# Turning the selected z by 32x32 blocks on VectorE, in a routed feed-forward kernel with split-precision products

## The chip, the cores and the metric

The kernel runs on one core of one Trainium2 chip. The metric is the device time of one execution in microseconds (us). The kernel before takes 426.58 us, the median of three runs (425.37 to 426.68).

## The reference, cut to what matters

```
W = weights[condition]                          # 64 matrices of 64 x 64, picked by index
y = einsum('bct,bcd->bdt', x, W)                # x: (64, 64, 1024), fp32
logits = y @ gate_w.T + expert_bias             # 4 experts
one_hot = one_hot(argmax(logits), 4)
z = einsum('nh,erh->ner', y, lora_A)            # 4 experts x rank 8 = 32 values for each row
delta = one_hot-selected (z @ lora_B[e].T)      # rank 8, the chosen expert alone
out = x + y @ W_up.T + delta
```

There are 4096 rows of 1024 values. For each row the kernel keeps of its 32 values of z the 8 of the best expert and sets the others to zero. The product with the four experts' `lora_B`, laid side by side as 32 rows, is then the delta.

## The kernel before, in words

**Tiling.** A tile is 128 rows, two batches of 64. A block q is two tiles, t = 0 and 1, and there are 16 blocks. Each block is a 2 x 2 x 2 product of halves (two tiles by two halves of the hidden size), done with seven products in place of eight, named after their stationary operand: a11, a12, a22, s2, s1, s3, s4. Each product is made with both operands split into a rounded high part and a low part, and three of the four part products are summed in PSUM, so a product has 12 matmuls of 512 columns or 24 of half as many. In the odd blocks the product a22 is itself split into seven quarter products, which take a22 of the even block before with them (`q1` to `q4`, and `q_of_sum` for 5, 6 and 7).

**Who does what.** TensorE makes y of the next block (`make_y`, L785) and the products (L869, L1071). ScalarE moves y out of PSUM (L524) and rounds the high parts (L533). GpSimd forms sums of operands (L304 to L317). VectorE forms the low parts (L289, and L1427 for quarter products), adds the products to x (L1264, L1268, L1458), and routes. SyncE loads and stores.

**Routing.** The gate's 4 columns and `lora_A`'s 32 are carried as extra columns in four products. When the tile's 36 columns are there, VectorE runs `route(q, t)`: `find_best` (L1221), `rank_best` (L1225), `find_first` (L1230), `select_z` (L1234, which writes `z_sel`, 128 rows x 32). `high_z` (L1247) writes the rounded z to parts 0 and 2 of `z_parts`, and `low_z` (L1251) z less its high part to parts 1 and 3. Each step waits for the one before on the semaphore `route_step`. TensorE turns `z_parts` (128 x 128) into a PSUM bank in `turn_z` (L884), and ScalarE copies it to `z_t[t]` (`move_z` L611, in block 0 also `move_first_z` L601). `z_t[t]` is the stationary operand of the low-rank matmuls (L875): `delta11_of` and `delta12_of` for t = 0, `second_delta` for t = 1. This happens 32 times, once for each tile.

**What sets the order.** The order of each engine's instructions is written out by hand, and semaphores join the engines. Every engine runs its own list in order. The lists are `one` for block 1, `even` for blocks 2, 4, ..., 14, `odd` for blocks 3, 5, ..., 13 and `odd` with `closing` for block 15 (on TensorE `close`). Block 0 is written out by itself, since it is mixed with the preparation of the weights.

On TensorE an even block runs a11, a12, s2, y, the turn of t = 0, s1, delta11, y, s3, y, s4, delta12, the turn of t = 1, y, second_delta. An odd block runs a11, q2, a12, q1, q5, s2, q6, q3, y, s1, the turn of t = 0, q7, delta11, y, s3, q4, y, s4, delta12, the turn of t = 1, y, second_delta. The closing block runs the turn of t = 0 and `last_columns(0)` (L1147, with s4's first columns) after q3; then delta11, s3, q7, s1, the turn of t = 1, q4, second_delta, `last_columns(1)`.

On VectorE, in an odd block, these stand around `route(q, 0)`:

```
drain(3, g, bank_b, 1, 1, 6)
route(q, 0)
after_p6(q, 1)
low_quarter(7, g)
low_operand(dve, "s4", a12, q)
```

and in the closing block `route(q, 0)` is followed by `low_operand(dve, "s4", a12, q)`, and `route(q, 1)` by `drain(7, g, bank_c, 3, 1, 5)`. TensorE's q7 waits for `low_quarter(7)`, `last_columns(0)` for the low part of s4, and q4 for `drain(7)`.

In block 0 VectorE runs after `route(0, 0)` the low parts `low_sum(1, 3)`, a11, `low_sum(4, 3)` and `low_sum(1, 1)`, and TensorE's product s1 waits for both of the `low_sum(1, ...)`. GpSimd has then its own two low sums to finish and goes on to `add_s1` and `add_s2` of block 1, for which it waits on ScalarE's last copies of y, and one of these stands behind `move_first_z` in ScalarE's list.

Of the kernel before, what the change touches and what calls it, by code (L numbers as in the profile page):

```python
# [5 lines left out]
def adaln_ffn_kernel(  # L6
# [39 lines left out]
    P = 128  # L46
# [10 lines left out]
    WARM_UP = 62  # L57
    ROUTE_STEPS = 7
    assert C == D and 2 * D == P and HALF == BANK and O == T and BLOCKS % 2 == 0
# [9 lines left out]
    with ctx:  # L69
# [117 lines left out]
        route_step = sem("route_step")  # L187
        z_turned = sem("z_turned")
        z_ready = sem("z_ready")
        delta11 = sem("delta11")  # L190
# [318 lines left out]
        def _(act):  # L509
# [88 lines left out]

            def move_first_z(src):
                act.wait_ge(z_turned, 1)  # L600
                act.activation(z_t[0][:, :], src, ACT.Copy).then_inc(z_ready, 1)  # L601
# [5 lines left out]
            def move_z(q, par, t, bank):  # L607
                act.wait_ge(z_turned, 2 * q + t + 1)
                if not (isinstance(q, int) and q == 0):
                    act.wait_ge(delta22 if t else delta12, q)  # L610
                act.activation(z_t[t][:, :], bank[:, 0:P], ACT.Copy).then_inc(z_ready, 1)  # L611

# [65 lines left out]
            move_first_y(3, 1, a22)  # L678
            move_first_z(y_ps[:, 1, 0:P])
            act.wait_ge(low["s4"], 1)  # L680
            move_first_y(2, 1, a12)
            move_z(0, 0, 1, chains[1][:, 1, :])
            act.wait_ge(y_summed, Y_AT[2, 1])
# [24 lines left out]
            def one(q):  # L708
                load_x(q + 1, 0, 0)
                round_s1(q, True)  # L710
                round_s2(q, True)
                load_x(q + 1, 0, 1)
                round_s4(q, True)
                round_s3(q, True)
                move_z(q, 1, 0, bank_c[:, 0, :])
# [6 lines left out]
                move_z(q, 1, 1, chains[0][:, 1, :])  # L722
                round_fine(5)
                round_fine(7)
                round_fine(6)
                act.wait_ge(product_done["a22"], 2)
                act.wait_ge(rebuilt, 4)
                round_fine(4)
                move_y(q + 1, 1, 1, a22_even)

            def even(q, g):
                load_x(q + 1, 1, 0)
                round_s1(q, True)
                round_s2(q, True)
# [4 lines left out]
                move_z(q, 0, 0, bank_c[:, 0, :])  # L739
# [6 lines left out]
                move_z(q, 0, 1, chains[1][:, 1, :])  # L746
                move_y(q + 1, 1, 1, a22)

            def odd(q, g, closing):
# [14 lines left out]
                move_z(q, 1, 0, y_ps[:, 1, :])  # L764
                if not closing:
# [3 lines left out]
                    move_y(q + 1, 1, 0, a21)  # L769
                move_z(q, 1, 1, chains[0][:, 1, :])  # L770
                if not closing:
# [6 lines left out]
        def _(pe):  # L778
# [128 lines left out]
            def first_delta21():  # L907
                add_delta_pair(1, bank_x).then_inc(delta21, 1)

            def turn_second_z(q, pair):  # L910
                pe.wait_ge(c11_out, q + 1)
                turn_z(pair[:, 1, 0:P], q, 1)

# [78 lines left out]
            multiply_half("s3", 1, bank_x, False)  # L992
            wait_piece_read("b21", 2)
            turn_z(y_ps[:, 1, 0:P], 0, 0)
            wait_y_moved(3, 1)
# [8 lines left out]
            multiply("s1", 0, bank_b, True)  # L1004
            turn_second_z(0, bank_y)
            wait_sums(4, 0)
            wait_sums(4, 1)
            last_product(0, bank_x)
            pe.wait_ge(z_ready, 2)
            first_delta22()  # L1010
            pe.wait_ge(z_ready, 2)
            first_delta21()


            def one(q):
# [9 lines left out]
                make_y(q + 1, 0, 0, 0)  # L1025
                pe.wait_ge(p4_out, q)
                turn_z(bank_c[:, 0, 0:P], q, 0)
                pe.wait_ge(c22_out, q)
# [4 lines left out]
                multiply("s3", q, chain, False)  # L1033
                make_y(q + 1, 0, 1, 0)
                multiply("s4", q, bank_c, True)
                delta12_of(q)
                turn_second_z(q, pair)
                make_y(q + 1, 0, 1, 1)
# [3 lines left out]
            def even(q, g):  # L1042
# [7 lines left out]
                make_y(q + 1, 1, 0, 0)  # L1050
                pe.wait_ge(c12_out, q)
                turn_z(bank_c[:, 0, 0:P], q, 0)
                pe.wait_ge(c22_out, q)
# [4 lines left out]
                multiply("s3", q, chain, False)  # L1058
                make_y(q + 1, 1, 1, 0)
                multiply("s4", q, bank_c, True)  # L1060
                delta12_of(q)
                turn_second_z(q, pair)
                make_y(q + 1, 1, 1, 1)
# [51 lines left out]
            def odd(q, g, closing):  # L1115
# [7 lines left out]
                multiply("s1", q, bank_b, True)  # L1123
                pe.wait_ge(y_summed, 4 * q + 4)
                turn_z(y_ps[:, 1, 0:P], q, 0)
                pe.wait_ge(quarter_out, quarters(g, 6))
# [10 lines left out]
                delta12_of(q)  # L1137
                turn_second_z(q, pair)
                make_y(q + 1, 0, 1, 1)
# [3 lines left out]
            def last_columns(n):  # L1143
                dst, cols = y_ps[:, n, 0:QUARTER], slice(n * QUARTER, (n + 1) * QUARTER)
                for k in range(KH):
                    for a, b in ((0, 0), (0, 1), (1, 0)):
                        mm = pe.matmul(dst, hl["s4"][:, a, k, :], w_of["s4"][:, b, k, cols],  # L1147
                                       start=(k == 0 and a + b == 0), stop=False, skip_group_check=True)
                pe.wait_ge(z_ready, 2 * LAST + 1)
                add_delta(0, dst, lora_b_hl[:, BANK + n * QUARTER:BANK + (n + 1) * QUARTER]).then_inc(delta12, 1)  # L1150

            def close(q, g, chain, pair):
                pe.wait_ge(y_summed, 4 * q + 4)
                turn_z(y_ps[:, 1, 0:P], q, 0)
                pe.wait_ge(low["s4"], q + 1)
# [7 lines left out]
                multiply("s1", q, bank_b, True)  # L1163
                turn_second_z(q, pair)
                pe.wait_ge(quarter_out, quarters(g, 7))
# [9 lines left out]
        def _(dve):  # L1175
# [63 lines left out]

            def twice(z):  # L1240
                return z[:, :].unsqueeze(1).to_broadcast([P, 2, ER])
# [12 lines left out]
            def route(q, t, used=True):  # L1254
# [5 lines left out]
                high_z(n, used or t)  # L1260
                low_z(n)

# [16 lines left out]

            def after_p2(q, par, used=True):  # L1280
                score_p2(q, par)
                route(q, 0, used)

# [79 lines left out]
            score_p2(0, 0)  # L1363
            route(0, 0, False)
            low_sum(dve, 1, 3)
# [184 lines left out]
```

## Time and profile before

| | before |
|---|---|
| median of three runs | 426.58 us |
| lowest and highest | 425.37, 426.68 us |
| span of the profiled execution, first to last instruction | 423.9 us |
| whole time of the profiled execution | not reported apart; the median lies 2.7 us above the span |
| TensorE busy | 414.2 us, 3003 matmuls |
| VectorE busy | 280.3 us, 605 instructions |
| ScalarE busy | 146.0 us, 282 instructions |
| GpSimd busy | 137.3 us, 123 instructions |
| mean granted TensorE clock | 0.996 |

Busy time is the time in which the profile has at least one instruction of an engine at work. The times of instructions overlap: a matmul's record holds its whole way through the array, so the next one starts before it ends. The cost of a matmul in a stream is therefore the distance between two starts, not its duration.

### The profile page before, as it was taken

The page shows a single profiled execution, that of the slowest core. Times are in us where ns is not written, and L with a number is a line of the kernel's source. Part 1 is how long each engine was busy: PE and PEld are TensorE (multiplying, and loading weights), DVE is VectorE, ACT ScalarE, POOL GpSimd, SP SyncE. Part 2 cuts the span into 40 slices and gives each one's busy share as a digit, 9 for nine tenths or more (in the row PEclk, how much of TensorE's full clock was granted, in tenths as well). Part 3 has the DMA queues.
Part 4 walks back from the last instruction along what each step waited for, and adds up shares of the span by engine and source line. Part 5 has one row for each costly group of instructions (what it writes and reads, how often), then busy time and mean ns, then how long its engine had stood idle before and what let it go on. Part 6 is the DMA issues. An engine that isn't in the chain of part 4 may idle for free.

```text
span 423.9 us, 8776 instructions
## 1 busy us (share of the span) xinstructions
PE 414.2 (98%) x3003; PEld 393.6 (93%) x3003; DVE 280.3 (66%) x605; ACT 146.0 (34%) x282; POOL 137.3 (32%) x123
## 2 busy tenths in 40 slices
PE   7998999999999999999999999999999999999997
PEld 6897998999999999999999999999999999999996
DVE  4699668586756576474675656575764756856684
ACT  5795222433223242232333233232332323323320
POOL 1488215506204080312605053050802216050430
PEclk9899999999999999999999999999999999999999
DMA  8820230503114032321125021150322212240102
GB/s 269 302 65 2 89 117 26 178 27 106 67 57 159 26 107 100 105 76 74 56 99 176 28 102 38 65 179 25 105 97 82 99 55 75 99 177 29 49 26 100
DMA packets 20991, 39.36 MB, mean 93 GB/s; under 512 B 7494, under 2 KB 7750, under 8 KB 20970
## 3 DMA queue, kind: packets, MB, share of 16 engines
q1 hardware_dynamic: 17600, 27.40, 18.3%
q10 hardware_dynamic: 3370, 11.69, 8.1%
q8 instruction: 12, 0.20, 0.2%
q14 instruction: 9, 0.07, 0.1%
HBM read 22.30 MB, written 16.78 MB: 92 GB/s over the span
## 4 chain that ended last, share of the span: by engine, by line
PE 92%; DVE 3%; DMA 1%; ACT 1%; SPq 1%; issue 1%; POOL 1%; ACTq 0%; POOLq 0%
PE bank_y L869 21%; PE bank_x L869 21%; PE y_ps L785 11%; PE bank_b L869 10%; PE bank_c L869 10%; PE bank_c L1071 5%; PE bank_b L1071 4%; DMA x_sb<-in_x_dram 1%; PE bank_x L849 1%; PE y_ps L794 1%; PE bank_x L875 1%; PE bank_b L875 1%; PE bank_y L875 1%; PE bank_c L875 1%; PE y_ps L1147 1%
## 5 line engine op out<-in xcount | busy, mean ns | idle before, releaser
L524 ACT ACTIVATE a<-y_ps 128x512 f32<-128x512 f32 x49 | 29.3, 598 | 93.4 <-PE y_ps L785 93.4
L785 PE MATMUL y_ps<-cond_pair,x_sb 128*128 128x128 f32 x448 | 59.0, 274 | 0.0
L785 PEld LDWEIGHTS y_ps<-cond_pair,x_sb 128*128 128x128 f32 x448 | 54.7, 191 | 1.2
L869 PE MATMUL bank_y<-w_s,hl_s 128*128 128x292 f32 (+1 forms) x384 | 51.4, 289 | 0.0
L869 PE MATMUL bank_x<-w_a,hl_a 128*128 128x256 f32 (+1 forms) x384 | 50.9, 288 | 0.0
L869 PEld LDWEIGHTS bank_x<-w_a,hl_a 128*128 128x128 f32 x384 | 49.5, 188 | 0.3
L304 POOL TENSOR_TENSOR s_sum<-a 128x512 f32<-128x512 f32 x9 | 11.6, 1291 | 117.3 <-ACT a L524 115.1
L869 PEld LDWEIGHTS bank_y<-w_s,hl_s 128*128 128x128 f32 x384 | 49.2, 188 | 0.1
L869 PE MATMUL bank_b<-w_s,hl_s 128*128 128x512 f32 x192 | 47.9, 398 | 0.0
L869 PE MATMUL bank_y<-w_a,hl_a 128*128 128x292 f32 x360 | 47.7, 288 | 0.0
L869 PEld LDWEIGHTS bank_y<-w_a,hl_a 128*128 128x128 f32 x360 | 46.6, 188 | 0.3
L869 PE MATMUL bank_x<-w_s,hl_s 128*128 128x292 f32 x336 | 45.2, 290 | 0.4 <-DVE hl_s L289 0.4
L304 POOL TENSOR_TENSOR s_sum<-a,a_even 128x512 f32<-128x512 f32 x7 | 9.0, 1291 | 112.4 <-ACT a_even L524 112.4
L869 PE MATMUL bank_c<-w_s,hl_s 128*128 128x512 f32 x180 | 45.0, 398 | 0.0
L869 PEld LDWEIGHTS bank_x<-w_s,hl_s 128*128 128x128 f32 x336 | 43.0, 188 | 0.6 <-issue 0.6
L869 PEld LDWEIGHTS bank_b<-w_s,hl_s 128*128 128x128 f32 x192 | 35.0, 188 | 6.9
L869 PEld LDWEIGHTS bank_c<-w_s,hl_s 128*128 128x128 f32 x180 | 32.7, 188 | 6.6 <-issue 0.2
L289 DVE TENSOR_TENSOR hl_s<-s_sum,hl_s 128x512 fp32r<-128x512 f32 x30 | 36.3, 1246 | 1.2 <-ACT hl_s L533 1.2
L289 DVE TENSOR_TENSOR hl_a<-a,hl_a 128x512 fp32r<-128x512 f32 x31 | 21.3, 689 | 18.9 <-ACT hl_a L533 18.9
L533 ACT ACTIVATE hl_s<-s_sum 128x512 fp32r<-128x512 f32 x32 | 20.2, 634 | 34.1 <-POOL s_sum L304 24.7
L1264 DVE TENSOR_TENSOR x_sb<-bank_y,x_sb 128x512 f32<-128x512 f32 x40 | 27.3, 682 | 6.0 <-PE bank_y L875 4.8
L533 ACT ACTIVATE hl_s<-a 128x512 fp32r<-128x512 f32 x32 | 19.3, 628 | 33.4 <-POOL a L312 22.5
(187 smaller groups left out, 648.3 us busy)
## 6 DMA issues: line engine op xcount, KB each, us to landing
out_dram<-x_sb SPq DMA_DIRECT2D x63, 256.0 KB, 2.0
x_sb<-in_x_dram ACTq DMA_DIRECT2D x22, 512.0 KB, 3.5
x_sb<-in_x_dram SPq DMA_DIRECT2D x10, 512.0 KB, 3.4
w_raw<-in_L_ffn_W_up_dram SPq DMA_DIRECT2D x8, 512.0 KB, 6.3
cond_pair<-in_L_cond_weights_dram SPq DMA_DIRECT2D x64, 16.0 KB, 2.2
out_dram<-x_sb SPq DMA_DIRECT2D x2, 128.0 KB, 2.0
router_sb<-in_L_ffn_lora_A_dram ACTq DMA_DIRECT2D x1, 128.0 KB
lora_b_sb<-in_L_ffn_lora_B_dram SPq DMA_DIRECT2D x1, 128.0 KB, 4.9
```

The lines of the kernel that those rows point to most:

```text
L289: eng.tensor_tensor(hl[op][:, 1, :, :], by_k(src[:, :]), hl[op][:, 0, :, :].bitcast(fp32), ALU.subtract)\
L304: eng.tensor_tensor(s1_sum[:, :], a21[:, :], second[:, :], ALU.add).then_inc(s1_added, 1)
L524: act.activation(to[:, :], y_ps[:, h, :], ACT.Copy).then_inc(y_summed, 1)
L533: act.activation(hl[op][:, 0, :, :], src[:, :].rearrange("q (k n) -> q k n", n=P), ACT.Copy)\
L785: mm = pe.matmul(y_ps[:, h, k * P:(k + 1) * P], x_sb[:, 2 * par + t, (h * KH + k) * P:(h * KH + k + 1) * P], cond_pair[:, 2 * par + t, :], ...
L794: mm = pe.matmul(first_y_bank(t, h)[:, k * P:(k + 1) * P], x_sb[:, t, (h * KH + k) * P:(h * KH + k + 1) * P], cond_pair[:, t, :], start=Tr ...
L849: mm = pe.matmul(dst, hl[op][:, a, k, :], w_of[op][:, b, k, cols], start=(fresh and k == 0 and a + b == 0), stop=(k == KH - 1 and a == 1), ...
L869: mm = pe.matmul(dst, hl[op][:, a, k, :], w[:, b, k, cols], start=(fresh and k == 0 and a + b == 0), stop=(k == KH - 1 and a == 1), skip_g ...
L875: return pe.matmul(dst, z_t[t][:, :], src, start=False, stop=True, skip_group_check=True)
L1071: mm = pe.matmul(bank[:, 0, 0:QUARTER], left[:, a, k, :], right[:, b, k, :], start=(fresh and k == 0 and a + b == 0), stop=(k == 1 and a = ...
L1147: mm = pe.matmul(dst, hl["s4"][:, a, k, :], w_of["s4"][:, b, k, cols], start=(k == 0 and a + b == 0), stop=False, skip_group_check=True)
L1264: return dve.tensor_tensor(wide(x_part(par, t, half)), bank[:, :, 0:QUARTER], wide(x_part(par, t, half)), ALU.add)
```

## The change

The block `z_rows` (32 x 128) takes the place of `z_parts` (128 x 4 x 32). VectorE turns the four 32 x 32 blocks of `z_sel` into `z_rows`, one instruction each. It then copies `z_rows` to partitions 0 to 31 and 64 to 95 of `z_t[t]` and writes the difference to partitions 32 to 63 and 96 to 127. TensorE's transposes of z, ScalarE's copies and their two semaphores are gone. TensorE waits for `route_step` right before the low-rank matmuls. Two waits on a free bank that stood before a turn (`p4_out`, `c12_out`) stand now before the product s4, which writes the same bank.

```
-    ROUTE_STEPS = 7
+    ROUTE_STEPS = 8
...
-        z_parts = sb("z_parts", [P, 4, ER], fp32)
+        z_rows = sb("z_rows", [ER, P], fp32)
...
-            def turn_z(dst, q, t):
+            def wait_z(q, t):
                 pe.wait_ge(route_step, ROUTE_STEPS * (2 * q + t + 1))
-                pe.transpose(dst, z_parts[:, :, :].rearrange("p n q -> p (n q)"), ident[:, :]).then_inc(z_turned, 1)

             def delta11_of(q, pair):
-                pe.wait_ge(z_ready, 2 * q + 1)
+                wait_z(q, 0)
                 add_delta_pair(0, pair).then_inc(delta11, 1)
...
             def second_delta(q, chain):
-                pe.wait_ge(z_ready, 2 * q + 2)
+                wait_z(q, 1)
...
-            def high_z(n, used):
-                dve.wait_ge(route_step, ROUTE_STEPS * n + 5)
-                if used:
-                    dve.wait_ge(z_turned, n)
-                dve.tensor_copy(z_parts[:, 0:4:2, :].bitcast(fp32r), twice(z_sel)).then_inc(route_step, 1)
-
-            def low_z(n):
+            def z_part(t, n):
+                return z_t[t][n * ER:(n + 1) * ER, :]
+
+            def turn_z(n):
+                dve.wait_ge(route_step, ROUTE_STEPS * n + 5)
+                for i in range(P // ER):
+                    turned = dve.transpose(z_rows[:, i * ER:(i + 1) * ER], z_sel[i * ER:(i + 1) * ER, :])
+                turned.then_inc(route_step, 1)
+
+            def high_z(q, t, n):
                 dve.wait_ge(route_step, ROUTE_STEPS * n + 6)
-                dve.tensor_tensor(z_parts[:, 1:4:2, :], twice(z_sel), z_parts[:, 0:4:2, :], ALU.subtract)\
+                if not (isinstance(q, int) and q == 0):
+                    dve.wait_ge(delta22 if t else delta12, q)
+                dve.tensor_copy(z_part(t, 0), z_rows[:, :])
+                dve.tensor_copy(z_part(t, 2), z_rows[:, :]).then_inc(route_step, 1)
+
+            def low_z(t, n):
+                dve.wait_ge(route_step, ROUTE_STEPS * n + 7)
+                dve.tensor_tensor(z_part(t, 1), z_rows[:, :], z_part(t, 0).bitcast(fp32), ALU.subtract)
+                dve.tensor_tensor(z_part(t, 3), z_rows[:, :], z_part(t, 0).bitcast(fp32), ALU.subtract)\
                    .then_inc(route_step, 1)
```

The calls of `turn_z` on TensorE and of `move_z` and `move_first_z` on ScalarE are taken out, and `route` calls the new `turn_z` on VectorE between `select_z` and `high_z`.

## Rows read from the trace of the kernel before

**Rows 1.** The page: span, then busy time, share and instructions of each engine.

```profile
span 423.9 us, 8776 instructions
...
PE 414.2 (98%) x3003; PEld 393.6 (93%) x3003; DVE 280.3 (66%) x605; ACT 146.0 (34%) x282; POOL 137.3 (32%) x123
```

**Rows 2.** TensorE's waits: releaser, us in total, times, longest.

```profile
PE bank_x L884 <- DVE z_parts L1251: 1.1, 1, 1.1
...
PE bank_x L869 <- DVE hl_s L289: 0.4, 1, 0.4
```

**Rows 3.** Timeline, block 4 (even), TensorE: start, duration, engine, line, work.

```profile
135.39 1.05 PE L785 MATMUL y_ps<-cond_pair,x_sb 128*128 128x128 f32 x8
...
136.28 0.27 PE L884 MATMUL bank_c<-ident,z_parts 128*128 128x128 f32 x1
136.31 3.01 PE L869 MATMUL bank_b<-w_s,hl_s 128*128 128x512 f32 x12
```

**Rows 4.** Timeline, block 5 (odd), from y to q7 on both engines.

```profile
161.29 1.05 PE L785 MATMUL y_ps<-cond_pair,x_sb 128*128 128x128 f32 x8
...
162.10 3.01 PE L869 MATMUL bank_b<-w_s,hl_s 128*128 128x512 f32 x12
...
162.46 0.25 DVE L1234 SCALAR_TENSOR_TENSOR z_sel<-ranks,first,scores 128x32 f32<-128x32 f32 x1
162.75 0.20 DVE L1247 CAST z_parts<-z_sel 128x64 fp32r<-128x64 f32 x1
162.98 0.22 DVE L1251 TENSOR_TENSOR z_parts<-z_sel,z_parts 128x64 f32<-128x64 f32 x1
...
163.12 0.68 DVE L1264 TENSOR_TENSOR x_sb<-bank_y,x_sb 128x512 f32<-128x512 f32 x1
163.72 0.41 DVE L1427 TENSOR_TENSOR hl_q<-a_even,hl_q 128x256 fp32r<-128x256 f32 x1
...
164.98 0.96 PE L1071 MATMUL bank_c<-w_q,hl_q 128*128 128x256 f32 x6
```

**Rows 5.** Timeline, block 4 (even), the end of its second route.

```profile
145.36 0.22 DVE L1251 TENSOR_TENSOR z_parts<-z_sel,z_parts 128x64 f32<-128x64 f32 x1
...
147.37 0.69 DVE L1268 TENSOR_TENSOR x_sb<-bank_c,x_sb 128x512 f32<-128x512 f32 x1 [1.79 <-PE bank_c L875]
...
148.09 0.48 PE L875 MATMUL bank_x<-lora_b_hl,z_t 128*128 128x256 f32 x2
```

**Rows 6.** Timeline, block 0, from the first route to the product s1.

```profile
38.19 1.20 DVE L1247 CAST z_parts<-z_sel 128x64 fp32r<-128x64 f32 x1
...
40.14 3.00 PE L869 MATMUL bank_c<-w_s,hl_s 128*128 128x512 f32 x12
...
41.04 1.29 POOL L304 TENSOR_TENSOR s_sum<-a 128x512 f32<-128x512 f32 x1 [1.71 <-ACT a L528]
41.37 1.51 DVE L268 TENSOR_TENSOR w_s<-t_sb,w_s 128x512 fp32r<-128x512 f32 x1
...
43.44 2.91 PE L869 MATMUL bank_b<-w_s,hl_s 128*128 128x512 f32 x12
```

**Rows 7.** Timeline, block 1, the second route under GpSimd's sums.

```profile
73.22 1.17 DVE L1251 TENSOR_TENSOR z_parts<-z_sel,z_parts 128x64 f32<-128x64 f32 x1
...
74.54 0.30 PE L884 MATMUL bank_x<-ident,z_parts 128*128 128x128 f32 x1 [1.15 <-DVE z_parts L1251]
...
75.49 0.48 PE L875 MATMUL bank_y<-lora_b_hl,z_t 128*128 128x256 f32 x2
```

**Rows 8.** Timeline, block 15 (closing), the two places behind a route.

```profile
408.17 0.69 DVE L289 TENSOR_TENSOR hl_s<-a,hl_s 128x512 fp32r<-128x512 f32 x1
...
409.63 1.67 PE L1147 MATMUL y_ps<-w_s,hl_s 128*128 128x256 f32 x12
...
416.73 0.42 DVE L1458 TENSOR_TENSOR x_sb<-bank_c,x_sb 128x256 f32<-128x256 f32 x1
...
418.01 0.96 PE L1071 MATMUL bank_c<-w_a,hl_a 128*128 128x256 f32 x6
```

More of the change, by code:

```diff
@@ L187, in adaln_ffn_kernel @@
         route_step = sem("route_step")
-        z_turned = sem("z_turned")
-        z_ready = sem("z_ready")
         delta11 = sem("delta11")
@@ L605, in wait_all_turned @@
                 act.wait_ge(piece_stage[b][c], TURNED)
[L607 to L611, printed above, removed]
             act.wait_ge(ident_done, 1)
@@ L678, in _ @@
             move_first_y(3, 1, a22)
-            move_first_z(y_ps[:, 1, 0:P])
             act.wait_ge(low["s4"], 1)
             move_first_y(2, 1, a12)
-            move_z(0, 0, 1, chains[1][:, 1, :])
             act.wait_ge(y_summed, Y_AT[2, 1])
@@ L714, in one @@
                 round_s3(q, True)
-                move_z(q, 1, 0, bank_c[:, 0, :])
                 move_y(q + 1, 0, 0, a11)
@@ L721, in one @@
                 move_y(q + 1, 1, 0, a21)
-                move_z(q, 1, 1, chains[0][:, 1, :])
                 round_fine(5)
@@ L738, in even @@
                 round_even_a22(q, g)
-                move_z(q, 0, 0, bank_c[:, 0, :])
                 move_y(q + 1, 0, 0, a11)
@@ L745, in even @@
                 move_y(q + 1, 1, 0, a21)
-                move_z(q, 0, 1, chains[1][:, 1, :])
                 move_y(q + 1, 1, 1, a22)
@@ L763, in odd @@
                     round_a11(q + 1, True)
-                move_z(q, 1, 0, y_ps[:, 1, :])
                 if not closing:
@@ L769, in odd @@
                     move_y(q + 1, 1, 0, a21)
-                move_z(q, 1, 1, chains[0][:, 1, :])
                 if not closing:
@@ L908, in first_delta21 @@
                 add_delta_pair(1, bank_x).then_inc(delta21, 1)
-            def turn_second_z(q, pair):
-                pe.wait_ge(c11_out, q + 1)
-                turn_z(pair[:, 1, 0:P], q, 1)
             def warm_up(n, bank):
@@ L992, in _ @@
             multiply_half("s3", 1, bank_x, False)
-            wait_piece_read("b21", 2)
-            turn_z(y_ps[:, 1, 0:P], 0, 0)
             wait_y_moved(3, 1)
@@ L1004, in _ @@
             multiply("s1", 0, bank_b, True)
-            turn_second_z(0, bank_y)
             wait_sums(4, 0)
@@ L1008, in _ @@
             last_product(0, bank_x)
-            pe.wait_ge(z_ready, 2)
+            wait_z(0, 1)
             first_delta22()
-            pe.wait_ge(z_ready, 2)
             first_delta21()
@@ L1025, in one @@
                 make_y(q + 1, 0, 0, 0)
-                pe.wait_ge(p4_out, q)
-                turn_z(bank_c[:, 0, 0:P], q, 0)
                 pe.wait_ge(c22_out, q)
@@ L1034, in one @@
                 make_y(q + 1, 0, 1, 0)
+                pe.wait_ge(p4_out, q)
                 multiply("s4", q, bank_c, True)
                 delta12_of(q)
-                turn_second_z(q, pair)
                 make_y(q + 1, 0, 1, 1)
@@ L1050, in even @@
                 make_y(q + 1, 1, 0, 0)
-                pe.wait_ge(c12_out, q)
-                turn_z(bank_c[:, 0, 0:P], q, 0)
                 pe.wait_ge(c22_out, q)
@@ L1059, in even @@
                 make_y(q + 1, 1, 1, 0)
+                pe.wait_ge(c12_out, q)
                 multiply("s4", q, bank_c, True)
                 delta12_of(q)
-                turn_second_z(q, pair)
                 make_y(q + 1, 1, 1, 1)
@@ L1123, in odd @@
                 multiply("s1", q, bank_b, True)
-                pe.wait_ge(y_summed, 4 * q + 4)
-                turn_z(y_ps[:, 1, 0:P], q, 0)
                 pe.wait_ge(quarter_out, quarters(g, 6))
@@ L1137, in odd @@
                 delta12_of(q)
-                turn_second_z(q, pair)
                 make_y(q + 1, 0, 1, 1)
@@ L1148, in last_columns @@
                                        start=(k == 0 and a + b == 0), stop=False, skip_group_check=True)
-                pe.wait_ge(z_ready, 2 * LAST + 1)
+                wait_z(LAST, 0)
                 add_delta(0, dst, lora_b_hl[:, BANK + n * QUARTER:BANK + (n + 1) * QUARTER]).then_inc(delta12, 1)
@@ L1153, in close @@
                 pe.wait_ge(y_summed, 4 * q + 4)
-                turn_z(y_ps[:, 1, 0:P], q, 0)
                 pe.wait_ge(low["s4"], q + 1)
@@ L1163, in close @@
                 multiply("s1", q, bank_b, True)
-                turn_second_z(q, pair)
                 pe.wait_ge(quarter_out, quarters(g, 7))
@@ L1238, in select_z, with route @@
                     op0=ALU.is_equal, op1=ALU.mult).then_inc(route_step, 1)
-            def twice(z):
-                return z[:, :].unsqueeze(1).to_broadcast([P, 2, ER])
-            def high_z(n, used):
+            def z_part(t, n):
+                return z_t[t][n * ER:(n + 1) * ER, :]
+            def turn_z(n):
                 dve.wait_ge(route_step, ROUTE_STEPS * n + 5)
-                if used:
-                    dve.wait_ge(z_turned, n)
-                dve.tensor_copy(z_parts[:, 0:4:2, :].bitcast(fp32r), twice(z_sel)).then_inc(route_step, 1)
-            def low_z(n):
+                for i in range(P // ER):
+                    turned = dve.transpose(z_rows[:, i * ER:(i + 1) * ER], z_sel[i * ER:(i + 1) * ER, :])
+                turned.then_inc(route_step, 1)
+            def high_z(q, t, n):
                 dve.wait_ge(route_step, ROUTE_STEPS * n + 6)
-                dve.tensor_tensor(z_parts[:, 1:4:2, :], twice(z_sel), z_parts[:, 0:4:2, :], ALU.subtract)\
+                if not (isinstance(q, int) and q == 0):
[6 more added lines that the diff above has]
+                dve.tensor_tensor(z_part(t, 3), z_rows[:, :], z_part(t, 0).bitcast(fp32), ALU.subtract)\
                    .then_inc(route_step, 1)
-            def route(q, t, used=True):
+            def route(q, t):
                 n = 2 * q + t
@@ L1259, in route @@
                 select_z(n)
-                high_z(n, used or t)
-                low_z(n)
+                turn_z(n)
+                high_z(q, t, n)
+                low_z(t, n)
             def add_pair(bank, par, t, half):
@@ L1278, in score_p2, with after_p2 @@
                 score(chains[1 - par], partial)
-            def after_p2(q, par, used=True):
+            def after_p2(q, par):
                 score_p2(q, par)
-                route(q, 0, used)
+                route(q, 0)
             def after_p4(q, par):
@@ L1363, in _ @@
             score_p2(0, 0)
-            route(0, 0, False)
+            route(0, 0)
             low_sum(dve, 1, 3)
```

3 lines of the change are left out of this document (removed).

## Prediction

> **What bounds the kernel.** I read the page first. TensorE is busy 98% of the span, and no other engine more than 66% [rows 1]. TensorE's waits come next. Outside the loads of the start they are a few single ones, the longest 1.1 us at a turn of z in block 1 and 0.4 us at the start of block 2 [rows 2]. So in steady state TensorE never waits, and the time is its instruction stream. What leaves that stream is a gain, and what VectorE delivers too late is a loss that shows at once. The question is thus not how much VectorE has to do on average but how much room stands, in each kind of block, between the end of VectorE's work behind a route and TensorE's instruction that needs it. I read this from the timeline, one block of each kind. The six odd blocks repeat each other: q7 starts 3.69 us after the y before it in this one [rows 4], and so it does in the other five.
>
> **What TensorE saves.** In the odd block eight matmuls of y are followed directly by s1, and the starts lie 162.10 - 161.29 = 0.81 us apart [rows 4]. In the even block a turn stands between, and it is 136.31 - 135.39 = 0.92 us [rows 3]. A turn costs 0.11 us of the stream, though its record says 0.27. There are 32, so 3.5 us at most.
>
> **What ScalarE saves.** It loses 32 copies of z. It is not the bound, and y reaches the sums of the next block by a copy that stands behind no z copy in the loop's critical part, so I cost this at nothing except in blocks 0 and 1 (below). No DMA moves. The two bank waits that moved to s4 are on additions that VectorE does long before s4, hidden by the products s1 and s3.
>
> **What VectorE pays.** Removed for each route: the copy (its successor starts 162.98 - 162.75 = 0.23 us later) and the subtraction (163.12 - 162.98 = 0.14 us), 0.37 us in all [rows 4]. Added: four block turns, two copies and two subtractions, of 32 partitions each.
> - The subtraction took 0.22 us for 64 columns and 0.41 for 256 [rows 4], about 1 ns for a column, so 0.29 us for 128.
> - The copy took 0.20 us for 64 columns; for 128 it is 0.20 to 0.26, and I take 0.23.
> - No row shows a block turn. Its bounds are 0.15 us (hardly more than a fixed cost) and the 0.25 us of the 32-column `select_z`. I take 0.20, the copy's, the nearest single-input row.
> - Where an instruction waits for its predecessor the distance is its duration plus 0.03 to 0.04 us (0.23 against 0.20). Where it does not, the next starts some 0.08 us before the end (L1264: 0.60 us to its successor, duration 0.68) [rows 4].
>
> Which distance holds for the added ones is the main choice. The overlapping pairs in this trace all take the whole height of 128 partitions from partition 0. The added ones read or write 32 partitions at 0, 32, 64 or 96 in turn, so none of them resembles such a pair, and I take the distance with full duration. With it: 4 x 0.235 + 2 x 0.265 + 2 x 0.325 = 2.12 us, less 0.37, about **1.8 us more for each route**. With overlap at the six places without a wait (three turns, the second copy, the second subtraction, the instruction behind) it is 6 x 0.12 = 0.7 less, **1.1 us**. No copy or subtraction of 32 partitions can be shorter than 0.15, so below 0.7 us more it can hardly be: 4 x 0.07 + 0.19 + 2 x 0.15 + 0.3 = 1.07, less 0.37. Above, with turns of 0.25, it is 2.0, and I allow 2.3.
>
> The Trainium skill (VectorE: DVE Perf Modes, Two Vector instructions with no wait between them) says that an instruction whose input or output starts in another group of 32 partitions than the last one's starts only when all earlier Vector instructions have finished. No row of this trace shows it. By it the sum below is the one with 1.8, without it the one with 1.1.
>
> **Odd blocks (3 to 13, six).** Behind `route(q, 0)` stand after_p6 and `low_quarter(7)`, and TensorE's q7 waits for the latter. It ends at 163.72 + 0.41 = 164.13, and q7 starts at 164.98 [rows 4]. From the end of a VectorE instruction to the matmul that it releases it is 0.15 us (the turn in block 1 that waited: its input was there at 73.22 + 1.17 = 74.39, and its matmul started at 74.54 [rows 7]). So q7 can start at 164.28 + d, and against before it moves by d - 0.70. For d = 1.8 that is +1.10. The turn of t = 1 gives back 0.11. Six times 0.99 = **+5.9 us**. Behind it VectorE catches up: it waits over 1 us for the products s3 and s4 later in the block.
>
> **Even blocks (seven).** The second route ends at 145.5, its successor waits for TensorE until 147.37, and z is needed at 148.0 [rows 5]. With 1.8 more it ends at 147.3, and z is in time. Behind the first route VectorE is idle 1.7 us. So seven times two turns are saved: **-1.5 us**. The cover goes if d passes 2.3.
>
> **Closing block.** `last_columns(0)` waits for the low part of s4: 408.17 + 1.8 + 0.69 + 0.15 = 410.81 in place of 409.63, +1.18. The second route is followed by `drain(7)`, for which q4 waits: 416.73 + 1.18 + 1.8 + 0.42 + 0.15 = 420.28 in place of 418.01 [rows 8]. Both together **+2.3 us**.
>
> **Block 0.** TensorE no longer waits for z before s4, so s4 starts about 1.5 us sooner. But s1 needs four low parts that stand behind the route. There VectorE meets GpSimd: the copy took 1.20 us in place of 0.20, and a subtraction 1.51 in place of 0.68 beside GpSimd's sum [rows 6]. An instruction of VectorE that meets one of GpSimd's there waits until it is over, up to 1.29 us. ScalarE's copy of z no longer holds back the last y, so the two sums (from 41.04 before) come when GpSimd is done with its sums, at about 39.4 (the copy that waited for them ended at 38.19 + 1.20), right under the new copies and subtractions. The route then ends near 42.4, the four low parts (2.4 us) near 44.9, and s1 starts near 45.1 in place of 43.44: **+1.6 us**. Bounds: without meeting -0.5, with the block turns blocked too +2.5.
>
> **Block 1.** z of the second tile was late by 1.1 us under GpSimd's sums [rows 2, 7]. Now y goes first. The block turns run beside GpSimd's last sum, whose end let the subtraction go on at about 74.3, and two copies and two subtractions bring z to 75.4, where the low-rank matmuls stood before (75.49). The y behind it leaves sooner, which ends the 0.4 us wait of block 2 [rows 2]. With the first turn **-0.5 us**; +0.5 if the block turns are blocked.
>
> **The sum.** 5.9 - 1.5 + 2.3 + 1.6 - 0.5 = +7.8 us. The span of 423.9 would be 431.7. The median of the runs lies 2.7 us above that span, and I add the sum to the median: **434.4 us**, 1.8% slower.
>
> **Rivals.**
> 1. The added instructions overlap (d = 1.1). Odd blocks 6 x (0.40 - 0.11) = 1.7, even -1.5, closing 0.48 in the first place and 416.73 + 0.48 + 1.1 + 0.57 - 418.01 = 0.9 in all, block 0 about +1.2, block 1 -0.5: +1.8, **428.4 us**. For it speaks that overlap is the habit of this trace; against it the changing partitions.
> 2. Faster: VectorE's room is enough. It decides at d = 0.70, at `low_quarter(7)` before q7. Under it all 3.5 us come, and 0.4 from block 2: **422.7 us**. The average load (66%) speaks for it; the eight instructions in place of two speak against, since they would have to cost 0.13 us each.
> 3. GpSimd blocks the turns too, or they are dearer (d = 2.3): odd 6 x 1.49 = 8.9, even -1.5, closing 1.7 and 3.3, block 0 and 1 +3.0: +13.7, **440 us** at most; nearer 437 with d = 2.0.
> 4. The change does less than it says on TensorE, because a semaphore wait costs as much as a turn: then up to 3.5 us are missing from each case. Waits that are satisfied left no gap in [rows 4], so I give it no share of its own.
>
> **Chances.** The forecast 0.6, overlap 0.18, faster 0.1, dearer 0.12. The forecast spans 431 to 437, with block 0 unmet or worse. For 8 in 10 the range goes down over most of the overlap case and up into the dearer one: 426.8 to 438.5. A change of 0.3% (1.3 us) is about what a measurement can tell from none. Faster by more: 0.1. Within: 0.1, the lower tail of the overlap case. Slower by more: 0.8.
>
> **What would show it.** VectorE's instructions go from 605 to 797 and its busy time up by 32 x (4 x 0.20 + 2 x 0.23 + 2 x 0.29 - 0.42) = 45 us. TensorE gets a new wait in front of q7 in each of six odd blocks, some 1.2 us, put down to `low_quarter`, and two in the closing block. An odd and an even block together would take 0.99 - 0.22 = 0.8 us more. Wrong would be: no wait at q7 (then d is under 0.7), block turns starting 0.1 us apart (rival 1), or a wait at the low-rank matmuls of the loop.

## The result, and the profile after

The changed kernel takes 431.04 us (median of four runs, 430.73 to 432.0) against 426.11 us for the kernel before on the same chip. The ratio is 1.0127, with a 95% interval from 1.0098 to 1.0156: slower, by 4.2 to 6.6 us. The forecast was 434.4 us with a range from 426.8 to 438.5.

The page of the kernel after: span, busy time and instructions of each engine, against [rows 1].

```profile
span 429.2 us, 8828 instructions
...
PE 413.0 (96%) x2971; PEld 390.0 (91%) x2971; DVE 322.5 (75%) x797; ACT 138.3 (32%) x250; POOL 136.6 (32%) x123
```

TensorE has 32 instructions less and 1.2 us less busy time, in a span that is 5.3 us longer: it now waits. VectorE has the 192 further instructions and 42 us more.

TensorE's waits in the kernel after, against [rows 2]: the releaser, us in total, times, longest. Waits on loads in the first 20 us are left out here.

```profile
PE bank_c L1038 <- DVE hl_q L1398: 4.2, 6, 0.8
PE bank_b L849 <- DVE w_s L266: 1.9, 1, 1.9
PE bank_y L855 <- DVE z_t L1221: 1.6, 2, 0.9
...
PE y_ps L1111 <- DVE hl_s L287: 0.9, 1, 0.9
PE bank_c L1038 <- DVE x_sb L1429: 0.6, 1, 0.6
```

The first row is q7 waiting for `low_quarter(7)`, once in each of the six odd blocks. The second is s1 in block 0, the third the low-rank matmuls of block 0 and of block 1. The last two are the closing block, `last_columns(0)` and q4. Only the third row is a wait for z itself. All others wait for something that stands behind z in VectorE's queue.

The timeline of the kernel after, block 5 (odd), against [rows 4].

```profile
162.28 1.06 PE L765 MATMUL y_ps<-cond_pair,x_sb 128*128 128x128 f32 x8
...
163.09 3.01 PE L849 MATMUL bank_b<-w_s,hl_s 128*128 128x512 f32 x12
...
163.45 0.25 DVE L1196 SCALAR_TENSOR_TENSOR z_sel<-ranks,first,scores 128x32 f32<-128x32 f32 x1
163.74 0.84 DVE L1208 STREAM_TRANSPOSE z_rows<-z_sel 32x32 f32<-32x32 f32 x4
...
164.61 0.21 DVE L1215 CAST z_t<-z_rows 32x128 fp32r<-32x128 f32 x1
164.84 0.22 DVE L1216 CAST z_t<-z_rows 32x128 fp32r<-32x128 f32 x1
165.09 0.28 DVE L1220 TENSOR_TENSOR z_t<-z_rows,z_t 32x128 fp32r<-32x128 f32 x1
...
165.39 0.28 DVE L1221 TENSOR_TENSOR z_t<-z_rows,z_t 32x128 fp32r<-32x128 f32 x1
165.70 0.69 DVE L1235 TENSOR_TENSOR x_sb<-bank_y,x_sb 128x512 f32<-128x512 f32 x1
166.31 0.42 DVE L1398 TENSOR_TENSOR hl_q<-a_even,hl_q 128x256 fp32r<-128x256 f32 x1
...
166.78 0.98 PE L1038 MATMUL bank_c<-w_q,hl_q 128*128 128x256 f32 x6 [0.69 <-DVE hl_q L1398]
```

From the start after `select_z` to `after_p6` VectorE takes 165.70 - 163.74 = 1.96 us, against 163.12 - 162.75 = 0.37 before [rows 4]: **1.59 us more for each route**. q7 starts 166.78 - 162.28 = 4.50 us after y, against 3.69.

**Where the 5 us come from.** The first 33 us, up to the first half of s3 in block 0, are mostly loads and preparation. In the 13 profiles of this study they took between 32.6 and 35.9 us, whatever the kernel. So I count from the start of that matmul group (34.68 us in the profile before, 33.32 after). From there on, profiles of kernels with the same order in block 0 agree: s1 of block 0 starts at 10.34 to 10.36 us in six of them. Behind it one thing still varies, the clock (below). Starts of the product s1 in some blocks, and of the last matmul, in us from that point:

| kernel | s1, block 0 | s1, block 1 | s1, block 2 | s1, block 3 | s1, block 14 | s1, block 15 | last matmul |
|---|---|---|---|---|---|---|---|
| before | 8.76 | 27.70 | 51.96 | 77.75 | 349.95 | 380.56 | 386.07 |
| after | 10.34 | 30.70 | 53.90 | 79.58 | 354.80 | 386.52 | 392.79 |
| difference | +1.58 | +3.00 | +1.94 | +1.83 | +4.85 | +5.96 | +6.72 |

Block 0 loses 1.6 us at s1 and another 1.4 before block 1. Blocks 1 and 2 give 1.1 back. From block 2 to block 14 the loop loses 2.9, 0.48 us for an odd and an even block together. The last stretch loses 1.9. The sum is 6.7 us. The profile before had its common point 1.4 us later, so the two spans differ by 5.3 us, and the medians by 4.9. The same holds for most runs below: ten of twelve lie, against the kernel before, 0.4 to 2.9 us higher by this count than by the timed ratios. No run shows why. What a stage costs is therefore surer here than the sum of the stages.

### The profile page after: what moved, and what is told of

Same layout as the page of the kernel before. It is cut to its first block, busy times and chain, and to the rows that moved or that the text cites. A ratio compares the mean times of both kernels' runs of the same rounds, so it can differ in the third digit from the quotient of the medians.

```text
span 429.2 us, 8828 instructions
## 1 busy us (share of the span) xinstructions
PE 413.0 (96%) x2971; PEld 390.0 (91%) x2971; DVE 322.5 (75%) x797; ACT 138.3 (32%) x250; POOL 136.6 (32%) x123
## 4 chain that ended last, share of the span: by engine, by line
PE 84%; DVE 10%; DMA 2%; issue 2%; SPq 1%; ACT 0%; DVEq 0%
PE bank_y L849 21%; PE bank_x L849 21%; PE y_ps L765 10%; PE bank_c L849 9%; PE bank_b L849 7%; PE bank_c L1038 5%; PE bank_b L1038 3%; DVE z_rows L1208 1%; PE bank_x L829 1%; DMA w_raw<-in_L_ffn_W_up_dram 1%; DVE x_sb L1235 1%; DMA x_sb<-in_x_dram 1%; DVE z_sel L1196 1%; PE bank_x L855 1%; PE bank_y L855 1%
## 5 line engine op out<-in xcount | busy, mean ns | idle before, releaser
L765 PEld LDWEIGHTS y_ps<-cond_pair,x_sb 128*128 128x128 f32 x448 | 55.7, 191 | 1.1
L849 PE MATMUL bank_b<-w_s,hl_s 128*128 128x512 f32 x192 | 49.2, 406 | 1.9 <-DVE w_s L266 1.9
L1235 DVE TENSOR_TENSOR x_sb<-bank_x,x_sb 128x512 f32<-128x512 f32 x40 | 27.4, 684 | 3.0 <-PE bank_x L855 2.6
```

The lines of the kernel that those rows point to most:

```text
L765: mm = pe.matmul(y_ps[:, h, k * P:(k + 1) * P], x_sb[:, 2 * par + t, (h * KH + k) * P:(h * KH + k + 1) * P], cond_pair[:, 2 * par + t, :], ...
L849: mm = pe.matmul(dst, hl[op][:, a, k, :], w[:, b, k, cols], start=(fresh and k == 0 and a + b == 0), stop=(k == KH - 1 and a == 1), skip_g ...
L1235: return dve.tensor_tensor(wide(x_part(par, t, half)), bank[:, :, 0:QUARTER], wide(x_part(par, t, half)), ALU.add)
```

## The experiments

Two theories were put to the chip. **Queue:** the turn on TensorE was worth 0.11 us, and the loss lies in what stands behind the route in VectorE's order. **Load, or z itself:** VectorE is too busy, or z is late for its own matmuls, whatever the order. Each run was timed in five rounds beside the kernel before; the ratios are against that.

**The gain alone.** The kernel before, less the turns and ScalarE's copies; VectorE's instructions are unchanged. `z_t` stays an identity, so the low-rank part of the output is left out.

```
-                turn_z(bank_c[:, 0, 0:P], q, 0)
...
-                pe.wait_ge(z_ready, 2 * q + 1)
+                wait_z(q, 0)
...
-                act.activation(z_t[t][:, :], bank[:, 0:P], ACT.Copy).then_inc(z_ready, 1)
```

> The kernel before without TensorE's 32 turns of z and without ScalarE's copies; VectorE's work stays as before, and TensorE waits for it right before the low-rank matmuls. The low-rank part of the output is left out (the stationary tile keeps an identity). Theory (a turn costs 0.11 us of TensorE's stream): 3.5 us for 32 turns, and up to 1.5 us more in blocks 0 and 1, where TensorE waited for a turn: 421.5 to 422.7 us against 426.1, no wait before q7. Rival (a satisfied wait costs as much as the turn, so nothing is gained on TensorE): 425.5 us or more.

Measured: 422.37 against 426.74 us, ratio 0.9901 (0.9872 to 0.9930). An odd and an even block together, a pair, take 0.47 us less (s1 of block 2 to s1 of block 14 is 295.16 us, against 297.99, over six pairs), so **a turn is worth 0.12 us of the stream**, and the rival is out. But from the common point to the last matmul only 2.5 us were won, since s1 of block 0 came 0.9 us later than before the change, and s1 of block 1 2.4 us later. The median is thus as expected, but not by the way expected: blocks 0 and 1 lost time where a gain had been named. More on that under the clock.

**The price alone.** The kernel before, complete, and seven more VectorE instructions behind each route.

```
+            def extra(n):
+                for i in range(P // ER):
+                    turned = dve.transpose(z_rows[0:ER, i * ER:(i + 1) * ER], z_sel[i * ER:(i + 1) * ER, :])
+                turned.then_inc(extra_step, 1)
...
                 low_z(n)
+                extra(n)
```

> The kernel before, complete, and behind each route seven further VectorE instructions of the kind added by the change, into tiles that nothing reads: four block turns, two copies, one subtraction, 1.65 us by the changed kernel's own distances (the change adds a net 1.59). TensorE's turns stay, so this is the price without the gain. Theory (the loss is what stands behind the route): q7 starts 0.95 us later in each of six odd blocks, the closing block loses 2 us, block 0 1.5 us or more: 434 to 436.5 us. Rival (the loss of the change is in the route's own result coming late to the low-rank matmuls, not in its successors): here z comes as early as before, so 426 to 427 us.

Measured: 437.05 us, ratio 1.0259 (1.0223 to 1.0295), somewhat above the expected range; the last matmul comes 11.7 us later than before the change, and 4.2 of them are lost by s1 of block 1. TensorE's waits in this run, less those of the start and those that the kernel before has too:

```profile
PE bank_c L1073 <- DVE hl_q L1443: 4.0, 6, 0.7
PE bank_b L871 <- issue: 2.4, 1, 2.4
...
PE y_ps L1149 <- DVE hl_s L291: 0.7, 1, 0.7
PE bank_c L1073 <- DVE x_sb L1474: 0.6, 1, 0.6
```

z itself does not wait for the added instructions here, and yet the wait at q7 and the two of the closing block are there as in the changed kernel. They belong to the queue and not to z. The second row is s1 of block 0. A pair of blocks takes 0.89 us more (303.30 against 297.99 over six). With the gain of 0.47 taken off, 0.42 remain, and the changed kernel has 0.48 (300.90 over six).

**The order in the odd blocks.**

```
                 drain(3, g, bank_b, 1, 1, 6)
+                low_quarter(7, g)
                 route(q, 0)
                 after_p6(q, 1)
-                low_quarter(7, g)
                 low_operand(dve, "s4", a12, q)
                 low_operand(dve, "s3", a21, q)
```

> The changed kernel, but in the six odd blocks of the loop the low part for q7 is formed before the route in place of behind it. Theory (q7 waits for what stands behind the route, 0.7 us in each of six): the six waits go, 4.2 us: 426.5 to 427.3 us against 431.0. Rival (VectorE is simply too busy there, so that something else behind the route, u2 or the low part of s3, is late in its place): 429.5 to 431 us, with a new wait of some 0.5 us before s3 or the low-rank matmuls in each odd block.

Measured: 428.99 us, ratio 1.0052 (1.0028 to 1.0075). The wait before q7 is gone, and the last matmul comes 3.6 us sooner than in the changed kernel. But a pair takes 49.55 us (297.30 over six), and the gain alone had 49.19. The time lies between the two forecasts, and both theories were half right. The timeline, block 5:

```profile
168.84 1.06 PE L765 MATMUL y_ps<-cond_pair,x_sb 128*128 128x128 f32 x8
...
170.03 3.25 PE L849 MATMUL bank_y<-w_s,hl_s 128*128 128x292 f32 x24
```

s3 now started 1.19 us behind y, where it is 0.81 without a wait. The next instruction in the queue, the low part of s3, had become the late one, hidden until then by the wait at q7. So the two low parts were swapped as well:

```
                 low_quarter(7, g)
                 route(q, 0)
                 after_p6(q, 1)
-                low_operand(dve, "s4", a12, q)
                 low_operand(dve, "s3", a21, q)
+                low_operand(dve, "s4", a12, q)
```

> As odd_order, and the low part of s3 is formed ahead of that of s4 (s3 is the earlier product on TensorE). In odd_order s3 started 1.19 us behind the y before it, 0.38 us later than before the change. Theory (that was the next instruction in VectorE's queue, late by what the route costs more): s3 starts 0.81 us behind y, and an odd and an even block together take 49.2 us as in the run without turns, against 49.55: 2.2 us less than odd_order over six pairs. Rival (ScalarE, which waits for the low part of s4 before it moves the next y, is now late): the wait moves to the s4 product or the next y, nothing is won.

Measured: 425.93 against 425.82 us, ratio 0.9986 (0.9956 to 1.0015). The timeline of TensorE in block 5:

```profile
168.26 1.06 PE L765 MATMUL y_ps<-cond_pair,x_sb 128*128 128x128 f32 x8
169.07 3.26 PE L849 MATMUL bank_y<-w_s,hl_s 128*128 128x292 f32 x24
```

s3 follows y after 0.81 us, and the pair takes 49.20 us (s1 of block 2 at 55.19, of block 14 at 350.37), the same as with the gain alone. **In the loop, the whole loss was the order.** VectorE does all of its added work in this run. Against it the changed kernel takes 50.15 us for a pair, so the wait recorded as 0.69 us at q7 cost 0.95 us of the stream. The median of odd_deadline is no lower than that of the kernel before, since block 0 and the closing block still lose.

**The closing block**, on top of the first order:

```
+                    low_operand(dve, "s4", a12, q)
                     route(q, 0)
-                    low_operand(dve, "s4", a12, q)
                     after_p6(q, 1)
+                    low_operand(dve, "s3", a21, q)
                     drain(6, g, bank_c, 1, 1, 0)
                     drain(3, g, bank_b, 1, 1, 6)
-                    low_operand(dve, "s3", a21, q)
...
+                    drain(7, g, bank_c, 3, 1, 5)
                     route(q, 1)
-                    drain(7, g, bank_c, 3, 1, 5)
```

> As odd_order, and in the closing block the low part of s4 goes before the first route, the low part of s3 ahead of two drains, and the drain of q7 before the second route. Theory: a further 1.5 to 2 us, since both waits of the closing block (0.9 and 0.6 us) go: 424.8 to 425.6 us. Rival (the closing block's end is set by z itself, which then comes later): no more than 0.5 us below odd_order.

Measured: 427.33 us, ratio 1.0035 (1.0006 to 1.0064), not as low as expected, since odd_order itself had stayed above its forecast; below odd_order it is 1.7 us. Both waits of the closing block are gone, and from s1 of block 14 to the last matmul it takes 36.81 us, against 38.02 in odd_order and 36.12 before: 1.2 us won. Two smaller waits came in their place, for the low part of s3 and for the addition of s1's product:

```profile
PE bank_y L849 <- DVE hl_s L287: 0.3, 1, 0.3
...
PE bank_b L855 <- DVE x_sb L1239: 0.2, 1, 0.2
```

**A control:** the same two edits in the kernel before.

> A control: the kernel before with the order of all_order in the odd and closing blocks. Theory: nothing there was late before the change, so 425.8 to 426.4 us, the same within 0.3%. Rival (the order is better by itself, so that all_order's gain says nothing on the change): 1 us or more faster.

Measured: ratio 1.0018 (1.0000 to 1.0035), and the last matmul at 386.09 against 386.07 us. This order is worth nothing by itself. It is worth something only once the route is longer. The swap of s3 and s4 and the order of block 0 (below) were not tried in the kernel before.

**Why a turn of VectorE costs what it does.**

```
-                    turned = dve.transpose(z_rows[:, i * ER:(i + 1) * ER], z_sel[i * ER:(i + 1) * ER, :])
+                    turned = dve.transpose(z_rows[:, i * ER:(i + 1) * ER], z_sel[0:ER, :])
```

> The changed kernel, but all four block turns read the first 32 partitions of the selected z (so the z of the other three quarters of the rows is left out); outputs as before. Theory (an instruction that reads from other partitions than the last one is held until that one is done): the distance between two turns falls from 0.21 us to about 0.12 us, each route is 0.3 us shorter, the wait before q7 falls from 0.7 to 0.4 us, and the time by 6 x 0.3 + 0.9 for blocks 0 and 15 = 2.5 us to about 428.5 us. Rival (the distance is a property of the turn, whatever it reads): 0.21 us and 431 us as before.

Measured: 427.89 us, ratio 1.0048 (1.0023 to 1.0073). The timeline of VectorE in block 3 of this run, and its wait at q7:

```profile
115.98 0.48 DVE L1208 STREAM_TRANSPOSE z_rows<-z_sel 32x32 f32<-32x32 f32 x4
116.49 0.21 DVE L1215 CAST z_t<-z_rows 32x128 fp32r<-32x128 f32 x1
```

```profile
PE bank_c L1038 <- DVE hl_q L1398: 2.0, 6, 0.4
```

Four turns take 0.48 us together in place of 0.84. The median record of one is 0.157 us (0.156 to 0.201 over the 128), against 0.200 in the changed kernel, so two starts lie about 0.1 us apart in place of 0.21. The only thing that changed is from which partitions they read. The Trainium skill's rule (VectorE: DVE Perf Modes, Two Vector instructions with no wait between them), by which an instruction whose input or output starts in another group of 32 partitions waits until all earlier ones have finished, agrees with these two numbers. It agrees too with the copies and subtractions, which start as late after each other as if each waited for the last (0.23 to 0.31 us) although three of these four distances have no wait on VectorE in them; that was not tried apart.

**Block 0 and the clock.** VectorE and GpSimd in block 0 of the kernel after:

```profile
37.96 1.29 POOL L302 TENSOR_TENSOR s_sum<-a 128x512 f32<-128x512 f32 x1
38.08 1.24 DVE L1216 CAST z_t<-z_rows 32x128 fp32r<-32x128 f32 x1
...
39.38 1.39 POOL L306 TENSOR_TENSOR s_sum<-s_sum,a 128x512 f32<-128x512 f32 x1
39.65 1.27 DVE L1221 TENSOR_TENSOR z_t<-z_rows,z_t 32x128 fp32r<-32x128 f32 x1
```

The second copy and the second subtraction end when GpSimd's sums end, 1 us late each. The gain alone shows the same without any added work on VectorE: there a subtraction of the route took 1.24 us and the low part of a11 1.77 us, since y and with it GpSimd's sums come sooner. So a loss of 0.9 us at s1 comes from what was taken off TensorE and ScalarE alone; with the added work it is 1.6.

The product s1 of block 0 waited 1.9 us, and then its 12 matmuls took 4.28 us, where they took 2.91 before. The windows of TensorE's stretches around it in the kernel after: busy time and count of each engine, the granted clock (1.00 is 2.4 GHz, 0.50 is 1.2 GHz), DMA share, GB/s.

```profile
33.00:41.00 8.00, 6.93 (x45) 6.13 (x45) 7.66 (x17) 4.12 (x8) 7.63 (x6) 1.00 0.00 1
41.00:43.70 2.70, 0.76 (x4) 0.47 (x4) 2.70 (x6) 0.00 (x0) 0.00 (x0) 1.00 0.00 0
43.70:47.70 4.00, 4.00 (x12) 3.17 (x13) 3.55 (x14) 0.00 (x0) 0.00 (x0) 0.67 0.17 66
47.70:51.40 3.70, 3.70 (x29) 3.62 (x28) 1.43 (x3) 0.22 (x1) 0.00 (x0) 0.90 0.21 75
```

After 2.7 us with 0.76 us of work the granted clock falls, and s1 and the next product run at a mean of 0.67 and 0.90 of it. In the same stretches of the kernel before it stays at 1.00. To test this, matmuls on zeros were put where TensorE idles:

```
             delta12_of(0)
+            wait_piece_read("b21", 2)
+            warm_up(18, y_ps[:, 1, :])
             wait_y_moved(2, 1)
```

> The changed kernel, with 18 matmuls on zeros into a free bank between the low-rank matmuls of block 0 and the product s1, where TensorE idles 1.95 us. Theory (the idle time before s1 lets the granted clock fall, which makes s1 and the start of the next product slow): the clock stays at full speed, s1 takes 2.8 us in place of 4.1 us, and the time falls by 1.2 to 1.6 us to about 429.6 us. Rival (s1 is slow there for another reason, VectorE's reads of PSUM or the first stores): s1 still takes 4 us, and the time is 431 us or more.

Measured: 432.11 us, ratio 1.0149 (1.0128 to 1.0171), slower than the change alone, against the theory. Each of the 18 ran as two, and they ended 1.8 us after s1 could have started. s1 itself took 2.99 us. So with 8:

> As fill, with 8 matmuls on zeros in place of 18, since each of the 18 was issued as two and they ran 1.8 us past the point where s1 could start. Theory: s1 starts where it did in the changed kernel (10.3 us behind the start of s2's first half in block 0), takes 2.8 us at the full clock, and s1 of block 1 comes at 29.2 in place of 30.7: 1.3 to 1.5 us faster than the changed kernel. Rival (8 are too few to keep the clock up): s1 again takes over 3.5 us, nothing is won.

Measured: 430.43 us, ratio 1.0111 (1.0072 to 1.0151). The timeline of TensorE and two windows of this run:

```profile
42.23 1.95 PE L891 MATMUL y_ps<-zeros 128*128 128x128 f32 x16
44.34 3.01 PE L849 MATMUL bank_b<-w_s,hl_s 128*128 128x512 f32 x12 [0.17 <-issue]
47.19 3.04 PE L849 MATMUL bank_x<-w_a,hl_a 128*128 128x256 f32 x24
```

```profile
43.00:46.00 3.00, 2.83 (x18) 2.41 (x17) 2.89 (x9) 0.00 (x0) 0.00 (x0) 1.00 0.00 0
46.00:49.00 3.00, 3.00 (x22) 2.75 (x21) 2.73 (x10) 0.00 (x0) 0.00 (x0) 1.00 0.23 87
```

s1 starts at the same place (10.36 us from the common point, which is the first half of s3 and not of s2, against 10.34), at full clock, and s1 of block 1 comes at 29.19 in place of 30.70. **The idle time costs 1.5 us of clock on top of itself.** Timed, the kernel is 0.7 us below the changed one by the ratios to before, and the intervals overlap, so the median neither shows nor denies it; the trace does, up to the last matmul (391.27 against 392.79). The clock's price is not the same each time. In the profile of odd_deadline the clock was 0.89 in the 2.7 us with the same wait, then 0.50 for 4 us and 0.70 for 3.7 us, and s1 of block 1 came at 31.99. The gain alone has it too (2.3 us of idle time, then 4 us at 0.62): s4 no longer waits for the turn, starts 1.45 us sooner, and TensorE arrives at s1 too early.

The cure of the wait itself is the order in block 0:

```
+            low_sum(dve, 1, 1)
+            low_sum(dve, 1, 3)
             score_p2(0, 0)
             route(0, 0)
-            low_sum(dve, 1, 3)
+            low_sum(dve, 4, 3)
+            after_p7(0, 0)
             low_operand(dve, "a11", a11, 1)
-            low_sum(dve, 4, 3)
-            low_sum(dve, 1, 1)
-            after_p7(0, 0)
...
-            delta11_of(0, bank_y)
-            delta12_of(0)
             wait_y_moved(2, 1)
...
             multiply("s1", 0, bank_b, True)
+            delta11_of(0, bank_y)
+            delta12_of(0)
```

> The changed kernel, but in block 0 VectorE forms the two low parts that s1 waits for before the first route, and TensorE does s1 before the low-rank matmuls of the first tile. Theory (the low parts behind the route hold s1 back by 1.6 us, and the idle time costs another 1.3 us of clock): s1 starts right behind s4, 3 us are won: 427.5 to 428.5 us. Rival (z is the bottleneck of block 0 in any order): the low-rank matmuls wait in place of s1, and less than 1 us is won.

Measured: 429.50 us, ratio 1.0090 (1.0071 to 1.0109). s1 starts at 6.75 us from the common point in place of 10.34 and follows s4 without a wait. Of the 3.6 us, 2.1 are left at block 1 (28.58 in place of 30.70), less than expected. New waits took the rest and what the clock gave back: 0.8 us for the sum that frees the bank and 1.5 us before the low-rank matmuls of the second tile, for the addition of s1's product, which stood behind the second route.

**All of it together:** the order of odd_deadline, the closing block's, and block 0 with the addition of s1's product ahead of the second route and the low part of a11 behind it.

> The changed kernel with the order of odd_deadline, that of all_order in the closing block, and in block 0 the order of block0 with the addition of s1's product ahead of the second route. Theory: all waits behind a route are gone but some 2 us in blocks 0 and 1, and the turns' 0.43 us in each pair remain as gain: 423 to 424.5 us, 0.4 to 0.8% faster than the kernel before. Rival (the gains do not add, since a block that is sooner done waits for loads or stores of x): 425.5 us or more.

Measured: **422.67 us against 425.82, ratio 0.9927 (0.9902 to 0.9952)**, faster than both kernels, and a little below the expected range. TensorE's waits in this run, behind the loads of the start:

```profile
PE bank_y L855 <- DVE z_t L1221: 0.9, 1, 0.9
PE bank_b L855 <- DVE z_t L1221: 0.6, 1, 0.6
PE bank_x L849 <- DVE x_sb L1235: 0.5, 1, 0.5
```

These stand in blocks 0 and 1; in the closing block the two small ones of all_order are left. A pair takes 49.19 us (295.16 over six), as with the gain alone. The last matmul comes at 382.97 us from the common point, 3.1 before the kernel before and 9.8 before the changed one, with the same instructions as the latter.

## Why the prediction was right, and where it was off

- **What bounds the kernel:** as put. What TensorE waited for VectorE in the loop was lost (0.95 us a pair for a wait of 0.69), the turns that left its stream were won once that wait was gone (odd_deadline), and VectorE's average load (75%) decided nothing.
- **The turn, 0.11 us:** 0.12 measured.
- **The price of a route, 1.8 us:** 1.59. The choice of the distance with full duration was right (the block turns' experiment). The terms were a little large: turns 0.21 us apart in place of 0.235, copies 0.23 to 0.25 in place of 0.265, subtractions 0.30 to 0.31 in place of 0.325.
- **Odd blocks, +1.10 at q7 and 0.99 in all:** +0.81 and +0.70 (4.50 - 3.69, less the second turn). This is the term of the sum that was mis-sized most: 0.2 us from the route, and 0.1 from the release, which took 166.78 - 166.73 = 0.05 us and not the 0.15 of [rows 7]. Six times 0.29 make 1.7 us, and a pair costs 0.48 us in place of the 0.8 named as a sign. The wait at q7 was 0.69 us, not 1.2. The claim that VectorE catches up behind q7 held only behind the wait: the low part of s3 had no room either, as odd_order showed.
- **Even blocks, -0.22 each:** -0.22 too, as the pair's 0.48 less the 0.70 of the odd block. One of the two turns is seen alone from s1 of an even block to s1 of the next odd one, 25.65 against 25.79. No new wait, as forecast.
- **Closing block, +2.3:** two waits at the places named, 0.85 and 0.65 us, and 1.9 us from s1 of block 14 to the last matmul.
- **Block 0, +1.6 at s1:** +1.58, by the mechanism named: two of the four new copies and subtractions met GpSimd's sums. s4 started 1.45 us sooner, against 1.5 forecast.
- **Missed: the clock.** The idle time before s1 was costed as time alone, 1.6 us against before. By block 1 the loss was 3.0 us. What the clock takes belonged in the sum as a term of its own.
- **Blocks 1 and 2, -0.5:** -1.1, with the wait of 0.4 us at block 2 gone as forecast, and z 0.9 us late in place of 1.1.

Together the steps give 6.7 us on the trace against 7.8 forecast, and the medians differ by 4.9. That the trace's sum is so near is in part luck, since the errors have both signs: the loop was overpriced by 1.7 us, and the clock, which was not in the sum, made up 1.4 of it. The rivals fall: overlap (1.1 us for a route) by the distance of 0.21, the faster one by the wait at q7, the costlier by 1.59.

## What to carry to other kernels

When work moves to an engine that has room on average, look at what stands behind it in that engine's queue, and order the queue by when each result is needed; here the same instructions in another order are 2% faster (the two ratios to the kernel before). After one late instruction is moved, the next one in the queue may be late, hidden until then by the first wait. Short work on 32 partitions in turn is dear on VectorE: eight instructions took 1.96 us, where two on 128 partitions, with a turn on TensorE and a copy on ScalarE beside them, took 0.37.

## What the runs showed of the hardware that had not been expected

- TensorE's granted clock fell from 1.00 to a mean of 0.67 (0.50 in another run) over the 4 us that followed 2.7 us with 0.76 us of work. The kernel without turns lost 2.4 us up to block 1: 0.9 where VectorE met GpSimd, and 1.5 behind the idle time at s1, 2.3 us long. The kernel before had idled for 0.9 us ahead of s4 and not at s1. Whether a later s4 would have kept the clock up was not tried.
- A block turn is not held up by GpSimd where a copy is. In block 1 of the kernel after, the four turns took their usual 0.84 us under GpSimd's sum, and the copy behind them 0.48 us in place of 0.21:

```profile
69.97 5.77 POOL L463 TENSOR_TENSOR rebuilt_b<-rebuilt_b 128x512 f32<-128x512 f32 x4 [13.74 <-DVE rebuilt_b L1351]
...
74.46 0.84 DVE L1208 STREAM_TRANSPOSE z_rows<-z_sel 32x32 f32<-32x32 f32 x4
...
75.33 0.48 DVE L1215 CAST z_t<-z_rows 32x128 fp32r<-32x128 f32 x1
```

- A transpose on TensorE whose record says 0.27 us costs the stream 0.12 us.
